# Sparse expert stages: the down products of a chunk two slots behind its up products instead of three

## The reference, cut to what matters

```python
# round 3 (in the kernel F2): the routed part
for e in range(E):
    expert_out = jax.nn.silu(flat @ w1_routed[e]) @ w2_routed[e]
    routed_out = routed_out + cw[:, e:e + 1] * expert_out
# round 4 (in the kernel F3)
for i in range(E):
    h = jax.nn.silu(x @ w1[i]) * (x @ w3[i])
    out = out + (h @ w2[i]) * wi[..., None]
```

## Time and profile before

| | |
|---|---|
| median of 3 runs | 1469.68 us (1468.7 to 1470.14) |
| the profiled execution, its own time | 1482.8 us |
| its span | 1481.1 us |
| PE busy, share of the span | 1274.2 us, 86% |
| PE weight loads | 1102.0 us, 74% |
| DVE | 1030.5 us, 70% |
| ACT | 832.8 us, 56% |
| POOL | 579.4 us, 39% |
| mean granted clock of PE | 0.946 |

### The profile page before, as it was taken

One profiled execution on the slowest core, in us unless ns is written; L12 is line 12 of the kernel. 1 busy time (PEld: TensorE's weight loads), 2 busy tenths in 40 slices (PEclk: granted clock), 3 DMA queues, 4 the chain that ended last, 5 costly groups with the idle time before them and its releaser, 6 DMA issues. The chain is left out here.

```text
span 1481.1 us, 24418 instructions
## 1 busy us (share of the span) xinstructions
PE 1274.2 (86%) x7846; PEld 1102.0 (74%) x7846; DVE 1030.5 (70%) x2300; ACT 832.8 (56%) x1716; POOL 579.4 (39%) x946
## 2 busy tenths in 40 slices
PE   4899898899999999989858993789999999936993
PEld 3788676787888888778747892678888788826993
DVE  4776689797766666867754664777777777744775
ACT  3456776666555555555535772566666666623562
POOL 7333622313075565112550453322544344431443
PEclk7899999999999999989978996999999999967997
DMA  4221141149455554011033997900000000017994
GB/s 114 69 58 45 41 161 63 33 106 184 71 194 196 195 200 167 23 50 44 21 94 126 322 342 153 167 1 1 1 12 5 1 15 1 12 39 265 382 390 150
DMA packets 97582, 167.18 MB, mean 113 GB/s; under 512 B 12849, under 2 KB 65003, under 8 KB 91695
## 3 DMA queue, kind: packets, MB, share of 16 engines
q1 hardware_dynamic: 92463, 157.13, 36.1%
q0 software_dynamic: 4992, 8.48, 1.6%
HBM read 104.21 MB, written 52.33 MB: 106 GB/s over the span
## 5 line engine op out<-in xcount | busy, mean ns | idle before, releaser
L1064 POOL TENSOR_SCALAR shared<-shared,xrd 128x589 f32<-128x589 f32 x128 | 98.2, 767 | 216.6 <-DVE xrd L1851 216.1
L1989 PE MATMUL psum<-xh,wl 128*128 128x512 f32 (+1 forms) x424 | 163.4, 385 | 5.7 <-ACT act_out L1221 2.4
L1747 DVE TENSOR_TENSOR hhl<-psum,hhl 128x512 fp32r<-128x512 f32 x208 | 141.9, 684 | 32.9 <-ACT hhl L1233 29.7
L1990 PE MATMUL psum<-xl,wh 128*128 128x512 f32 (+1 forms) x432 | 161.6, 374 | 0.3 <-issue 0.3
L1991 PE MATMUL psum<-xh,wh 128*128 128x512 f32 (+1 forms) x432 | 161.8, 375 | 0.0
L1743 DVE TENSOR_TENSOR psum<-act_out,psum 128x512 f32<-128x512 f32 x128 | 88.9, 696 | 84.2 <-PE psum L1991 75.0
L1297 ACT ACTIVATE hhl<-psum 128x512 fp32r<-128x512 f32 (+1 forms) x160 | 95.3, 595 | 91.2 <-PE psum L2379 88.8
L1221 ACT ACTIVATE act_out<-psum 128x512 f32<-128x512 f32 x128 | 76.5, 598 | 117.9 <-PE psum L1991 117.5
L1856 DVE TENSOR_TENSOR hhl<-psum,hhl 128x512 fp32r<-128x512 f32 (+1 forms) x160 | 109.8, 687 | 28.4 <-ACT hhl L1297 26.1
L1233 ACT ACTIVATE hhl<-psum 128x512 fp32r<-128x512 f32 x208 | 123.2, 593 | 2.2 <-DVE psum L1743 2.1
L1289 ACT ACTIVATE shared<-psum,xnm 128x589 f32<-128x589 f32 x128 | 96.2, 751 | 32.8 <-DVE xnm L1845 31.3
(11 more groups left out here) (381 smaller groups left out, 3967.6 us busy)
## 6 DMA issues: line engine op xcount, KB each, us to landing
xs_dram<-aw SPq DMA_DIRECT2D x4, 4615.0 KB
parts_dram<-shared SPq DMA_DIRECT2D x8, 1536.0 KB, 6.5
wh<-parts_dram SPq DMA_DIRECT2D x24, 512.0 KB
wl<-parts_dram SPq DMA_DIRECT2D x23, 512.0 KB
parts_dram<-shared SPq DMA_DIRECT2D x9, 1024.0 KB, 5.2
ab<-parts_dram SPq DMA_DIRECT2D x8, 1024.0 KB
wh<-parts_dram SPq DMA_DIRECT2D x8, 1024.0 KB
kb<-parts_dram SPq DMA_DIRECT2D x14, 512.0 KB
```

The lines of the kernel that those rows point to most:

```text
L1064: g.tensor_scalar(xprob[m % XS], xprob[m % XS], xrd[:, z], 1.0, ALU.mult, ALU.mult).then_inc(x_norm, 1)
L1747: v.tensor_tensor(hl[k % 4], h_bank(f, k), hh[k % 4].bitcast(f32), ALU.subtract).then_inc(f.h_ready, 1)
L1989: mm(dst, ll, rh, start=start, stop=False)
L1990: mm(dst, lh, rl, start=False, stop=False)
```

## The change

Each of the two sparse stages gets a field `lag` of 2, and PE's loop puts `block_down(k - 2)` into slot k instead of `block_down(k - 3)`. Nothing else differs: the programs of ACT, DVE, POOL and SP, all waits and all buffers are the same. The dense stages keep LAG = 3.

```diff
@@ -392,6 +392,7 @@
         F2.up_cols, F3.up_cols = 1024, 2048
         F2.second, F3.second = 0, 4
+        F2.lag, F3.lag = 2, 2
         FFNS = [F0, F1, F2]
@@ -2480,8 +2481,8 @@
                 for k in range(last + 4):
                     if k < last:
                         block_up(k)
-                    if LAG <= k < last + LAG:
-                        block_down(k - LAG)
+                    if f.lag <= k < last + f.lag:
+                        block_down(k - f.lag)
                     if k % 2 == 0 and k // 2 + 2 < NBLK:
                         block_in(k // 2 + 2)
                     if k % 2 and k >= 5:
```

## The result

The change makes the kernel slower: 1520.11 us (1516.22 to 1521.36, 4 runs) against 1469.19 us (1468.63 to 1470.14, 4 runs) for the kernel before. The ratio is 1.0341, with a 95% interval of 1.0322 to 1.0361. The forecast was 1518.9 us.

A forecast was written before the change was run, and what follows sets the result against it. PE's program was taken to bound both sparse stages. F2's 29.2 and F3's 22.5 us, less 2.5 given back, made +49.2: 1482.8 to 1532.0 us profiled, less 13.1 without the profiler, 1518.9 us (+3.3%), range 1509 to 1532.

The forecast's parts named there:

- The bound: Stages F2 and F3: both last as long as PE's program, PE busy 9.56 and 10.00 of 10 us.
- The wait for the bank: First down product waits for `result(s - 1)` in the same slot: +1.39 us a block in F2, +1.07 in F3.
- the signs: Changed trace: some 20 waits a stage for `result` before the down products, 35 and 21 us in all; clock 1.00.
- The sum: 21 blocks in each stage: F2 29.2 us, F3 22.5, together 51.7, less 2.5 given back: +49.2 us.
- Given back in fill and end: Start and end of F2 and F3: 1.0 us in the fills plus 1.55 at the ends, 2.5 in all.
- The chunk's own data, costed at nothing: Down products' wait for `b_lo` of chunk k - 2, steady part: 0 us, covered by a slot of PE's work.
- The clock: Both stages: full clock taken; rival of a quarter at the lower level adds 31 us, about 1550, chance 7%.
- The transfers: Both stages: transfers get easier, costed at nothing; rival that they set the pace, 1467 to 1470 us, chance 3%.
- From the profiled execution to the median: Whole kernel: runs without the profiler lie 13.1 us lower, carried over, taking 1532.0 to 1518.9 us.

The follow-up runs named there:

- the control: Kernel before with lag 3 kept, ScalarE's `high` moved ahead of `func` or `gate`, `result` still behind: 1462.61 us, ratio 0.9970; run again 1462.53 us, 0.9968.
- the run with `result` first: The change (lag 2, both stages, one bank) with `result` put first in ScalarE's even slots: 1473.58 us, ratio 1.0042 to the kernel before.
- the run with two banks: Kernel before with lag 2 in F2 only and F2's sums in two PSUM banks in turn: 1472.31 us, ratio 1.0037.

## Why the prediction was right

**The bound.** PE's program is the length of both stages. Right: in the four kernels whose pace moved by 0.5 us a block or more in a stage, 21 times the change of the pace gives the change of the time within 2 us. For the smaller differences it doesn't hold so well, with the pace from one execution: the second run of the control has the pace of before in its profile and a median 5 us lower.

**The wait for the bank.** The step that carried the forecast was that `result(s - 1)` now stands in the same slot as the product that waits for it. The down products were put at 2.47 us after the slot's start in F2 and 2.48 in F3, and come at 2.47 and 2.46. Taking the wait away by a second bank leaves 0.37% of F2's 1.95%, taking it away by an order leaves 6 of the 51 us, and taking one of the three ScalarE instructions out of the chain takes out that instruction's step. Of the signs, the waits were to read 1.7 and 1.0 us, 35 and 21 us in all; they read 1.5 and 0.8, 32.5 and 17.4, because the view's brackets leave out the 0.16 to 0.18 us that lie below the row before, while the forecast counted from start to start.

**The sum.** +1.39 and +1.07 us a block were forecast; 1.32 and 1.03 came. The block of F2 shown above takes 5.05 us, the mean one 5.02, and the forecast had 5.09: the 1.83 us from `block_in` on were read from a block in which `block_in` had stood, after which its own row is 0.44 us long instead of 0.38, and here it is 1.80. Given back in fill and end were 1.8 us in F2 and 0.8 in F3 by the forecast. F2 gave back 0.8 (21 x 1.32 = 27.8 against 27.0), F3 1.7 (21 x 1.03 = 21.6 against 19.9): the sum of both is right, its parts are not. In the fill of F2 the first down products wait for `low`, the only such wait on PE in this stage:

```profile
796.43 0.36 PE L2474 MATMUL psum<-hhl,wh 128*128 128x256 f32 x1 [0.87 <-DVE hhl L1916]
```

**The chunk's own data, costed at nothing.** This step was right for the change and wrong in its reason. "The cover is a whole slot of PE's work" is not so: in F2 PE comes to the down products 2.44 us after the up products of the slot before began (837.61 to 840.05 in the run with `result` first), while the chain of `func`, `high` and `low` that those up products start lets them begin after 2.96 (840.57). ScalarE begins `func` of a slot only when those products end, 1.0 us after they began, and `high` and `low` of the chunk before it stand behind that. The wait is there, 0.34 to 0.36 us by the bracket in each even slot, and it is hidden behind the longer one. By itself the lag of 2 costs F2 0.18 us a block, some 4 us, and the time of the run with two banks is higher by a ratio of 1.0037 (1.0017 to 1.0058), 5 us. A reader of the prediction would have expected that mending the bank brings the kernel to 1466; it was expected so for two runs, and both missed by this term. In F3, with 36 up and down products a block instead of 24, the step holds: in the run with `result` first PE has no such wait in the steady part of F3.

**The clock.** It was taken at full, and the rule of the Trainium skill ("TensorE: Matmul & The Clock Gate", section "A second HAM failure mode: psum-queue depth-cycling") spoke against it. Its case is another kernel, with bf16 data and 512 columns. What it describes did not come about here: with one gap of 1.5 us in each block of F2 and PE 7.04 of 10 us busy, the granted clock is 1.00, and products start 0.12 apart.

**The transfers.** They did not set the pace, as said: 3.42 us a block is reached in F2 with the same transfers.

**From the profiled execution to the median.** The 13.1 us were carried over as they were. The two profiled executions stand +13.6 and -3.9 us to their medians, so the forecast of the profiled one (1532.0) is 16 us off while that of the median is 1 us off. That the latter is so close is in part luck: the stages themselves gained 46.9 us, not 49.2.

## What to carry to other kernels

Before an instruction is moved ahead in one engine's program, look at each of its waits, and find in which place of the other engine's program the releaser stands and what that place waits for. If the releaser stands behind something that waits for the moved instruction's own slot, the two engines take turns, and the price is the chain between them. Read it from start to start in the trace before; the brackets of idle time are shorter, and a wait of 0.30 us had none at all. When such a wait is mended, the next one is right behind it, so work out the second as well. Here it was worth more to order the helper engine's work by what it already has in hand (`result` and `high` before the `func` that must wait) than to change the distance.

## What the runs showed of the hardware

A gap of 1.5 us on PE in each 5.0 us, with 7.04 of 10 us busy, did not lower its clock in F2, nor did one of 0.8 us in each 5.7 us, with 9.22 of 10 us busy, in F3. ScalarE's copies and Silus of 512 columns take 0.59 us but start 0.48 to 0.50 us after each other, so a chain of three of them costs less than the sum of their times. A matmul that had to wait for such a copy began 0.10 to 0.11 us after its end. At 3.3 us a block, with 372 GB/s and a DMA share of 1.02, single loads came late in F2, by 0.4 us, and by up to 2.0 us in the control. The rate alone does not decide it: F3 of the kernel before had 373 GB/s at the same share, and PE was busy for all of the 10 us.
